# When GpSimd writes its two lists of single elements: the first behind a counting loop, the second whole behind the weighted sums

## The reference, cut to what matters

```
L0: three GCN layers:  out = segment_sum(h[src] * dinv[src] * dinv[dst], dst) + b, with self loops
L1: attention over edges (GATv2, 4 heads): softmax of scores per dst, then a weighted segment_sum
L2: SAGE, two layers:  mean over incoming edges @ Wl + bl + x @ Wr
L3: two layers, mean over OUTGOING edges: segment_sum(h[dst], src) / degree, @ W, relu
```

## Time and profile before

| what | value |
|---|---|
| median of 3 runs | 6769.15 us (6765.42 to 6769.48) |
| span of the profiled execution (the page gives no time of its own beside it) | 6773.4 us |
| busy in the span: PE, DVE, POOL, ACT | 3327.6, 2834.7, 2848.7, 1678.0 us |
| mean granted TensorE clock | 0.865 |
| moved by DMA | 931.28 MB, 137 GB/s |

### The profile page before, as it was taken

One profiled execution on the slowest core, in us unless ns is written; L12 is line 12 of the kernel. 1 busy time (PEld: TensorE's weight loads), 2 busy tenths in 40 slices (PEclk: granted clock), 3 DMA queues, 4 the chain that ended last, 5 costly groups with the idle time before them and its releaser, 6 DMA issues.

```text
span 6773.4 us, 61344 instructions
## 1 busy us (share of the span) xinstructions
PE 3327.6 (49%) x19159; PEld 3101.4 (46%) x19160; DVE 2834.7 (42%) x3813; ACT 1678.0 (25%) x2774; POOL 2848.7 (42%) x2780
## 2 busy tenths in 40 slices
PE   0000000000006999997444444427601999959697
PEld 0000000000005989997333334326601898959697
DVE  7000000000006454545766667679850443444345
ACT  0000000000003545453000000003310554636365
POOL 2776666667770000000677767736787000020200
PEclk9999999999998999998556565558955999979898
DMA  9691000000004858683333333215600754848686
GB/s 364 217 391 60 1 1 1 1 1 1 1 1 141 270 187 275 193 274 117 90 85 86 86 87 89 84 35 169 192 13 18 253 193 147 275 140 282 208 273 199
DMA packets 589168, 931.28 MB, mean 137 GB/s; under 512 B 99379, under 2 KB 359433, under 8 KB 582550
## 3 DMA queue, kind: packets, MB, share of 16 engines
q1 hardware_dynamic: 464722, 701.52, 32.8%
q10 hardware_dynamic: 42484, 162.22, 6.1%
q0 software_dynamic: 81744, 64.83, 4.1%
HBM read 692.69 MB, written 235.58 MB: 137 GB/s over the span
## 4 chain that ended last, share of the span: by engine, by line
PE 35%; another core or an unknown queue 34%; DVE 14%; issue 11%; POOL 2%; ACT 1%; DMA 1%; DVEq 1%; SPq 0%; ACTq 0%; POOLq 0%
PE banks L899 29%; PE banks L822 3%; POOL work L599 2%; DVE work L1496 1%; DVE Z L1391 1%; DVE Z L1394 1%; DVE Z L1396 1%; DVE big L1400 1%; DVE work L1187 1%; ACT X L644 1%; DVE V L1092 1%; DVE Z L1398 1%; DVE Z L1297 1%; DVE V L1093 0%
## 5 line engine op out<-in xcount | busy, mean ns | idle before, releaser
L899 PE MATMUL banks<-wides,rows 128*128 128x384 f32 (+2 forms) x11040 | 2043.2, 346 | 282.4 <-issue 153.9
L899 PEld LDWEIGHTS banks<-wides,rows 128*128 128x128 f32 x11040 | 1957.0, 190 | 363.0 <-issue 178.0
L599 POOL DMA_INDIRECT work<-tab,stage x832 | 896.4, 1077 | 1527.9 <-ACT stage L752 1264.7
L1258 DVE CAST wides<-big 128x768 fp32r<-128x768 f16 (+3 forms) x1429 | 811.6, 569 | 1348.6 <-PE banks L899 1069.8
L674 ACT CAST wides<-big 128x768 fp32r<-128x768 f16 (+2 forms) x1037 | 832.4, 805 | 675.4 <-PE banks L899 563.9
L844 PE MATMUL banks<-work 128*128 128x50 f16 x784 | 93.8, 278 | 1815.9 <-issue 1692.4
L569 POOL DMA_INDIRECT cells_b<-queue_i x784 | 816.2, 1041 | 303.7 <-issue 301.8
L844 PEld LDWEIGHTS banks<-work 128*128 128x128 f16 x784 | 73.2, 149 | 1836.5 <-issue 1710.0
L569 POOL DMA_INDIRECT cells<-queue_i x784 | 767.2, 979 | 319.4 <-issue 312.8
L1186 DVE TENSOR_TENSOR work<-big 128x400 f16<-128x400 f16 x98 | 36.0, 367 | 1814.3 <-remote 1663.0
L953 PE MATMUL banks<-V,work 128*128 x1664 | 368.0, 410 | 413.3 <-ACT work L754 334.0
(11 more groups left out here) (313 smaller groups left out, 3375.6 us busy)
## 6 DMA issues: line engine op xcount, KB each, us to landing
big<-cells SPq DMA_DIRECT2D x490, 416.0 KB
big<-cells SPq DMA_DIRECT2D x441, 384.0 KB
big<-cells_b SPq DMA_DIRECT2D x300, 384.0 KB
cells_b<-work ACTq DMA_DIRECT2D x50, 1600.0 KB
gathered<-work SPq DMA_DIRECT2D x104, 512.0 KB
work<-gathered SPq DMA_DIRECT2D x104, 512.0 KB, 5.0
big<-cells_b SPq DMA_DIRECT2D x100, 416.0 KB
cells<-work ACTq DMA_DIRECT2D x98, 416.0 KB, 14.7
```

What stands on the lines that cost most here:

```text
L599: pool.indirect_dma_start(msg[:, j, u, :], None, tab[0][:, :], bass.IndirectOffsetOnAxis(ap=stage[:, j * U + u:j * U + u + 1].bitcast(U32) ...
L899: last = pe.matmul(banks[:, 4 * (w % 2) + j, 0:(z - a) * P], rows2[:, s, part * D:(part + 1) * D], wides[:, q % QUEUE, (a - start) * P:(z ...
L1258: dve.tensor_copy(wides[:, (2 * m + 1) % QUEUE, 0:(z - a) * P], halves[:, m % HALVES, a * P:z * P]).then_inc(s_wided, 1)
```

## The change

The wait for the end of the counting loop is put ahead of the first list's piece 0. The first ten pieces of the second list leave their place behind the first list, and the whole second list, with its first fetch, follows the weighted sums. The integers that SyncE and GpSimd load once are now loaded by `bounded`, which is `registers` with the check of the bounds at run time left in.

```diff
-THEN = 10
@@
+        def bounded(engine, row, first, n, most):
+            return nc.values_load_multi_w_load_instructions(row[0:1, bass.ds(first, n)], engines=[engine], min_val=0, max_val=most)[1]
@@ SyncE
             sp.wait_ge(s_go, go("cuts"))
-            written = registers(mybir.EngineType.SP, ready_i, 0, len(FIRST) - 1, PIECES)
+            written = bounded(mybir.EngineType.SP, ready_i, 0, len(FIRST) - 1, PIECES)
@@ GpSimd
             fetch(0, 0)
             pool.wait_ge(s_go, go("cuts"))
-            zeroed = registers(mybir.EngineType.Pool, ready_i, len(FIRST) - 1, PIECES, len(FIRST))
+            zeroed = bounded(mybir.EngineType.Pool, ready_i, len(FIRST) - 1, PIECES, len(FIRST))
+            pool.wait_ge(s_cmm, STEPS + 2)
             scatter(0, cells, 0, 1)
@@
             pool.wait_ge(s_zero_b, 16 * CT)
-            pool.wait_ge(s_kept[1], 16)
-            fetch(1, 0)
-            scatter(1, cells_b, 0, THEN)
@@ behind the weighted sums
-            scatter(1, cells_b, THEN, PIECES)
+            pool.wait_ge(s_kept[1], 16)
+            fetch(1, 0)
+            scatter(1, cells_b, 0, PIECES)
```

## The result

The changed kernel takes **6723.11 us** (median of 4 runs, 6719.12 to 6726.31); the kernel before took 6767.28 us beside it (6762.36 to 6769.48). The ratio is 0.9937 [0.9923, 0.9951]: 44 us faster, where 149 were forecast. The direction held, and the time lies in the 8 in 10 range (6565 to 6745), but outside the forecast's own range of 6570 to 6690: the size of the gain is less than a third of the one forecast.

A forecast was written before the change was run, and what follows sets the result against it. GpSimd's element writes were taken to bound the kernel by delaying TensorE's completions. Terms -821 and +672 gave -149 on the profiled 6773.4, so 6624, adjusted to 6620 us; own range 6570 to 6690 (65 in 100), 8 in 10 range 6565 to 6745.

The forecast's parts named there:

- The reading of the chain: Counting loop: 22.4 us for two steps beside GpSimd's element writes, 1.065 us a step without; all 98 then take 104.4 us.
- rival 2: ScalarE's zeroing of the matrices, until just after 531 us, holds the counting loop, not the element writes: 6984 us; 8 in 100.
- rival 5: The counting loop is slow of itself, so the first list would start 2089 us late: some 8700 us; 1 in 100.
- rival 4: Small products ahead of layer 0 escape the delay and GpSimd loses nothing to VectorE: 6574 us; 7 in 100.
- rival 3: The strips done below the element writes bring nothing: 6701 us; 7 in 100.
- Part 1: First list waits for the count, runs from 253 to 1313 us, hiding 19 strips of layer 0: 821 us gained.
- Part 3: All 14 pieces of the second list behind the weighted sums: 723 us longer, less 51 for 32 layer 3 strips: +672.
- rival 1: GpSimd stays at 1.40 us a write in both lists: a change of -25 us, 6744 us; 12 in 100.
- GpSimd's 1568 writes are nearly exclusive time: Both lists: TensorE's completions come at 2.8 us per matmul during writes, so write duration and useful work hidden below count.
- The three windows of the earlier trace: GpSimd's write rates before: 1.407 us in the counting loop, 1.397 over the first list, 1.26 beside the dense pass.

The follow-up runs named there:

- 208-column kernel: Kernel before, order untouched, one memset of 208 columns on GpSimd behind each element write (a write every 1.451 us): 5551.85 us, 0.8226, chip 1.
- spacing runs: Kernel before with GpSimd memsets behind each element write: writes every 1.776, 1.56, 1.451, 1.386 us took 6045.65, 5671.39, 5551.85, 5935.58 us.
- kernel with bursts: Changed kernel with the second list split into four bursts, at dense passes 1 and 2, behind the weighted sums, at pass 4: 6546.38 us, chip 2; 6497.45, chip 1.
- changed order with 64 columns: Changed kernel with two memsets of 64 columns on GpSimd behind each element write: 6120.21 us, 0.9067 against the kernel before, chip 1.
- order of before, 128 columns: Kernel before, order untouched, one memset of 128 columns on GpSimd behind each element write: 5267.27 us, 1.0196, on chip 4.
- the list alone: Changed kernel, with VectorE waiting behind the count until the whole first list has landed, so no other engine works beside it: 6819.59 us, 1.0069, chip 2.

## Why the prediction was half right

**What held.** The reading of the chain: the counting loop was slow only because of the writes beside it (98 free steps; first write at 253.3; rival 2, the zeroing, and rival 5 fall, though the zeroing has a small part, as the 208-column kernel shows). The small products are held as well, 131 and 259 us for the 140 and 274 that 2.8 us each would give, so rival 4 falls. Strips go on below the writes at one in 22.4 us, so rival 3 falls. The rule of the Trainium skill that no DMA contends with a compute engine ("SBUF — State Buffer", section "Who interferes with whom") does not describe what the trace of the changed kernel shows, a strip in 22.4 us beside the writes and 1.57 alone. It fits chip 4, with 49 strips in 200 us beside them.

**The step that failed** is in Part 1, repeated in Part 3: "The list will now lie beside waiting engines and the dense pass, so I take 1.273". It measured 1.42 in the long run of both lists. In Part 1 the list took 1368 - 253 = 1115 us instead of 1060, and the dense pass was free at 1381 instead of 1323. Below it 27 strips were done instead of 19: the first stretch of matmuls had 42.7 of its 84.4 us left, so 42 us were hidden instead of 30. 58 less 12 is 46, all by which the gain fell short of 821. In Part 3 the end of the second list came 5250.7 - (5236.7 - 774.8) = 789 us after where the four pieces of before would have ended, instead of 723: 66 more. Less 2 us for the strips below it (53 us hidden instead of 51) and 10 for the shorter restart behind it, that is the 54 us by which the cost was under-estimated. So -149 became -49 in the span.

This was rival 1, put at 6744 with 12 in 100: at the rate of the count the sum was -25. Its lists have nearly the measured lengths (1125 and 788 us; measured 1115 and 789). The truth is somewhat better than its sum, as more strips were hidden, and the restart behind the second list was 10 us quicker. For the strips an error of the forecast helped: layer 0 began 47 us earlier than computed (839, not 886). The 148 small products cost 2.6 us each and not 2.8 (24 us less), and the 21 transposes were through in 34 us, not 59, since the first of them were not held. The time fell into the 8 in 10 range because that range took in part of rival 1, and not by the forecast's sum.

**Why the row misled.** The three windows of the earlier trace rows differ in two things: what runs beside them, and how far into a list they lie. I credited all of the difference to the first. The list with no engine beside it has the same 1.425 us, so it was all the second. A hint was in the same rows: 1016 / 727 and 788 / 560 are nearly equal, though only the first has the zeroing beside it.

**Where the 49 us come from.** The time under writes has not changed at all: 1908 (132 to 2040) + 338 (4899 to 5237) = 2246 us before, 1115 + 1131 = 2246 us after. What has changed is what it hides. Ahead of the first list 121 us now stand uncovered. Against that, layer 0 is under way 13 us after the list's end instead of 74 (61 us), 27 of its strips are done by then (42 us), 35 of layer 3 more than before (53 us), and the restart behind the second list is 10 us quicker: 166 - 121 = 45 of the 49. The other 4 lie between the two lists, where the way from the first landmark to the second list's first write takes 2694 us and not 2699.

**What the sum left out.** "GpSimd's 1568 writes are nearly exclusive time" was taken as given. By the spacing runs it is true only of writes issued faster than the row's own settled pace. Adding a pause of 0.17 us a write, with the order untouched, gives 1196 us on chip 1.

## What to carry to other kernels

When an engine's issue rate is read from a short window, look for a window as long as the stretch that you will price with it, and as deep into the row. If a long row of small DMAs holds back engines that share no data with it, first space the row out to just above its own settled pace; only then move it. Where there is no hold the pause is not free: on chip 4 one of 0.1 us a write cost 2% (5267 against 5166 us). And a reordering that pays because of such a hold can cost several per cent where the hold is absent: here a 0.6% gain on one kind of chip stands against an estimated 7% loss on another.

## What the runs showed of the hardware

- A long row of 128-element indirect writes of 2 bytes settles at 1.425 us a write, the fetches included, on chips 1 and 2 (1.27 to 1.29 for the first 200 to 330 writes), and stays at 1.27 to 1.28 on chip 4.
- Where the writes pile up, matmul completions reach VectorE and ScalarE at 2.6 to 2.8 us per matmul. The hold starts within 26 us of the first write beside the zeroing at 388 GB/s, some 90 us after it beside a dense pass at 273 GB/s (the kernel with bursts), and ends 5 to 25 us after the last. Of 50 single-column products TensorE starts 34 within 1.1 us and the others 2.8 us apart, so it is held too once some are outstanding.
- The same hold appears beside GpSimd's 50 row gathers ahead of pass 5, 1.26 us apart: waits of 10 to 16 us from 5391 us on in the changed order with 64 columns, 40 us after the last element write (one stands in its chain above). It also appears in the attention block, beside 832 gathers in groups of 8: there 27% of the changed kernel's chain has no known releaser, 25% in the kernel with 208 columns, and none on chip 4 (order of before, 128 columns); the gathers take 1265, 1240 and 1124 us. So the 5552 us still have a part of the hold in them, and no run spaced the gathers.
- The same kernel takes 5166 us on chip 4 and 6746 to 6769 on three others, at a mean granted clock of 0.80 to 0.83 there and 0.86 to 0.87 on chip 1: the clock does not explain it.

What stays open: where the pile sits (between GpSimd, the rings and the DMA engines no view tells), by what path it delays TensorE's completions, and why chip 4 shows no slower pace. That the pile is the cause rests on the spacing runs and on the list alone; its length was never seen directly.
